# Layer 1 with fp16 plane pairs: two of every four probability tiles transposed by DMA, their low planes made on GpSimd

## The chip, the cores and the metric

One core of a Trainium2 chip runs the whole kernel. The metric is the device time of one execution in microseconds; the kernel before has a median of 682.38 us over 3 runs (681.85 to 683.33). Engine names are those of the profile: PE is TensorE's matmul and PEld its weight load, DVE is VectorE, ACT is ScalarE, POOL is GpSimd, SP is SyncE, which issues the DMAs.

## What is computed

Four images x of 256 channels and 1024 pixels (32 x 32), all in float32. Layer 0 is a position attention with a residual; layer 1 is a group norm, an attention of 4 heads of 64 channels and a projection with a residual:

```python
# layer 0
S = softmax(einsum('bcn,bcm->bnm', Wb @ x, Wc @ x))          # 1024 x 1024 per image
y = gamma * einsum('bcm,bnm->bcn', Wd @ x, S) + x
# layer 1
hn = group_norm(y, 32 groups)
q, k, v = (w @ hn + b for w, b in ((wq, bq), (wk, bk), (wv, bv)))   # 4 heads x 64
attn = softmax(einsum('bhdq,bhdk->bhqk', q, k) * 64 ** -0.5)        # 1024 x 1024 per head
out = y + wp @ einsum('bhqk,bhdk->bhdq', attn, v) + bp
```

To keep float32 accuracy, every operand of a matmul is split into a high part and a low part, and a product is two or three matmuls on them.

## The kernel before

**Tiles.** Layer 0 has 8 tiles per image and layer 1 has 32 (4 heads x 8), each 128 queries by 1024 keys. A layer-1 image runs 32 steps. Tiles are ordered so that four tiles in a row (4j to 4j+3) are 512 queries of one head: they make half a head, and their values product av j is computed in steps 4j+4 to 4j+7, a quarter (four matmuls of 512 columns) per step.

**One tile in layer 1.** PE computes the scores into one of two PSUM buffers (`scores1`), two steps ahead. DVE takes the row maximum (`row_max`), ACT the exponential with the row sum (`exp`), DVE the reciprocal of the sum (`recip`), POOL multiplies the tile by it (`normalise`). PE transposes the tile in eight 128 x 128 pieces into the PSUM pair `trans` (`transpose_tile`), ACT copies it out as the high part (`trans_high`), DVE subtracts for the low part (`trans_low`). PE then multiplies both parts with the stacked values (`values`). In the kernel before these parts are `pt_hi` and `pt_lo` in float32r.

**Layer 0** already turns its tiles by DMA: POOL writes the high fp16 plane (`high_plane`), DVE the low one (`plane_low`), SP issues one DMA transpose per plane (`turn`), and ACT and DVE widen the result to `pt_hi` and `pt_lo`.

**Order.** There is no scheduler. Each engine executes its instructions in the order in which they are written in its block, and semaphores tie the engines together. In layer 1 the table `STEPS1` says which groups PE adds in which step: projections of q and k for the next image (`next_qk0` to `next_qk6`, `qk7`), of v (`v0` to `v3`), the output projection, and the av quarters. In a step s of layer 1 the order is:

- PE: scores of tile s+2 (they wait for exp of tile s), transposes of tile s, the groups of `STEPS1[s]`, the av quarter last.
- ACT: put away a finished av, `trans_high` of tile s, exp of tile s+2, other groups' high parts.
- DVE: reciprocal of tile s+1, other groups of step s-1, row maximum of tile s+2, `trans_low` of tile s, av of step s-1.
- POOL: normalise tile s+1, then pieces of the group norm or of an output split.
- SP: it restacks each finished q or k chunk with four DMAs (`restack`), loads and stores.

The line numbers in rows are those of the kernel before: L979 row maximum, L739 exp, L984 reciprocal, L626 normalise, L1444 transposes, L749 and L997 high and low part of a transposed tile, L1410 all matmuls, L466 restack, L478 and L481 the layer-0 DMA transposes.

Of the kernel before, what the change touches and what calls it, by code (L numbers as in the profile page):

```python
# [21 lines left out]
F32 = mybir.dt.float32  # L22
F32R = mybir.dt.float32r
# [5 lines left out]
P = 128  # L29
IMAGES = 4  # L30
C = 256
# [28 lines left out]
PARTS0_FIRST = ["d0", "d1", "d2", "d3", "av0", "av1", "next_a0", "next_a1", "next_a2", "next_a3"]  # L60
# [165 lines left out]
def halves_before(t1):  # L226

    return 2 * t1 - TILES_LAYER0
# [19 lines left out]
def build(nc, x, weights, vecs, out):  # L248
    y_dram = nc.dram_tensor("y_scratch", (IMAGES, KT, P, N), F32, kind="Internal").ap()
    ctx = ExitStack()  # L250
    with ctx:
# [36 lines left out]
        pt_hi = sb("pt_hi", [P, 2, NT, H], F32R)  # L288
        pt_lo = sb("pt_lo", [P, 2, NT, H], F32R)
# [26 lines left out]
        v_st = sb("v_st", [P, NT, HEADS, 2, HD], F32R)  # L316
# [66 lines left out]
        pool_steps = sem("pool_steps")  # L383

# [49 lines left out]
        def _(sp):  # L434
# [5 lines left out]
            def load_x(i):  # L440
                for half in range(X_HALVES):
# [1312 lines left out]
```

## Time and profile before

| | us |
|---|---|
| median of 3 runs | 682.38 |
| the profiled execution | 682.95 |
| its span, first to last instruction | 681.0 |
| PE busy | 668.9 (98%) |
| DVE busy | 560.4 (82%) |
| ACT busy | 455.7 (67%) |
| POOL busy | 231.2 (34%) |

Layer 0 ends and layer 1 begins at about 242 us. PE reads as busy nearly throughout because matmuls are pipelined: a 512-column float32r matmul is recorded as 390 ns, while the next one starts about 228 ns after it. How long PE really takes is therefore read from the starts in the timeline, and whether an engine sets the pace is read from the gaps between starts on the others. The granted TensorE clock is 1.00 (2.4 GHz) over the whole span.

### The profile page before, as it was taken

How to read it: one execution, taken by the hardware profiler on the slowest of the kernel's cores; microseconds unless marked ns; L12 is line 12 of the kernel's file. 1: busy time of each engine (PE TensorE's matmuls, PEld its weight loads, DVE VectorE, ACT ScalarE, POOL GpSimd, SP SyncE). 2: the span in 40 equal slices, each digit the busy share in tenths (PEclk: the TensorE clock that was granted, in tenths of full speed). 3: DMA queues.
4: the chain of work that ended last, by engine and by line, in shares of the span. 5: the costliest groups of instructions: out<-in, count | busy, mean ns of one | idle time of the engine just before them, and what ended most of it. 6: DMA issues, size and time to landing. Idle time of an engine off the chain costs nothing.

```text
span 681.0 us, 11125 instructions
## 1 busy us (share of the span) xinstructions
PE 668.9 (98%) x3668; PEld 568.5 (83%) x3668; DVE 560.4 (82%) x910; ACT 455.7 (67%) x790; POOL 231.2 (34%) x216
## 2 busy tenths in 40 slices
PE   8989999999999899999999999999999999999997
PEld 7878888888888778888888888888888888988886
DVE  4787768768678478998888899888899888889996
ACT  5563435435435167988787788777789778778884
POOL 0130211201125024565233465242546433334531
PEclk9999999999999999999999999999999999999999
DMA  7476856645645957001656010367110265301001
GB/s 227 85 134 188 170 99 138 155 100 128 165 97 123 213 141 203 1 1 48 146 119 185 17 47 1 93 155 193 54 54 8 58 157 126 92 16 47 1 32 62
DMA packets 96714, 69.50 MB, mean 102 GB/s; under 512 B 71072, under 2 KB 73376, under 8 KB 96672
## 3 DMA queue, kind: packets, MB, share of 16 engines
q1 hardware_dynamic: 96672, 68.97, 41.8%
q8 instruction: 22, 0.36, 0.2%
q14 instruction: 20, 0.16, 0.1%
HBM read 18.62 MB, written 8.39 MB: 40 GB/s over the span
## 4 chain that ended last, share of the span: by engine, by line
PE 86%; DVE 5%; issue 3%; ACT 2%; POOL 2%; DMA 1%; SPq 1%; POOLq 0%; DVEq 0%; ACTq 0%
PE acc L1410 36%; PE scores L1410 26%; PE trans L1444 16%; PE trans L1410 8%; DVE negmax L979 1%; ACT prob L739 1%; DMA x_raw<-in_x 1%; POOL planes L638 1%; DVE pt_lo L997 1%; ACT pt_hi L749 1%; DVE pt_lo L1168 1%; DMA turned<-planes 0%; POOL y_in L649 0%; SPq L466 0%; DVE qk L1132 0%
## 5 line engine op out<-in xcount | busy, mean ns | idle before, releaser
L626 POOL TENSOR_SCALAR prob<-prob,rsum 128x1024 f32<-128x1024 f32 x127 | 142.8, 1124 | 256.7 <-DVE rsum L984 256.7
L739 ACT ACTIVATE prob<-scores,negmax 128x1024 f32<-128x1024 f32 x160 | 178.9, 1118 | 74.4 <-DVE negmax L979 72.9
L979 DVE TENSOR_REDUCE negmax<-scores 128x1 f32<-128x1024 f32 x160 | 194.0, 1213 | 17.8 <-PE scores L1410 16.6
L749 ACT ACTIVATE pt_hi<-trans 128x512 fp32r<-128x512 f32 x256 | 139.6, 594 | 63.9 <-PE trans L1444 63.3
L997 DVE TENSOR_TENSOR pt_lo<-trans,pt_hi 128x512 fp32r<-128x512 f32 x256 | 163.5, 680 | 1.0 <-ACT pt_hi L749 0.6
L1410 PE MATMUL scores<-k_st,q_st 128*128 128x512 f32 x512 | 137.9, 391 | 0.7 <-issue 0.7
L1444 PEld LDWEIGHTS trans<-ident,prob 128*128 128x128 f32 x1024 | 117.7, 140 | 22.5 <-issue 4.2
L1444 PE MATMUL trans<-ident,prob 128*128 128x128 f32 x1024 | 134.6, 273 | 1.2 <-DVE pt_lo L997 1.1
L1410 PEld LDWEIGHTS scores<-k_st,q_st 128*128 128x128 f32 x512 | 95.7, 188 | 21.6 <-issue 1.2
L1410 PE MATMUL acc<-pt_hi,v_st 128*128 128x512 f32 (+1 forms) x264 | 106.8, 407 | 0.6 <-DVE pt_lo L997 0.6
L1410 PE MATMUL acc<-pt_lo,v_st 128*128 128x512 f32 (+1 forms) x264 | 101.0, 385 | 0.0
L638 POOL TENSOR_SCALAR planes<-prob,rsum 128x1024 f16<-128x1024 f32 x32 | 36.7, 1146 | 164.9 <-DVE rsum L984 161.6
L1410 PEld LDWEIGHTS acc<-pt_hi,v_st 128*128 128x128 f32 x264 | 49.8, 189 | 7.8 <-DVE pt_lo L997 0.8
L812 ACT ACTIVATE pt_hi<-turned 128x1024 fp32r<-128x1024 f16 x32 | 33.8, 1057 | 33.3 <-DMA turned<-planes 33.3
L1410 PEld LDWEIGHTS acc<-pt_lo,v_st 128*128 128x128 f32 x264 | 49.9, 189 | 7.1
L984 DVE RECIPROCAL rsum<-rowsum 128x1 f32<-128x1 f32 x160 | 25.8, 161 | 31.8 <-ACT prob L739 27.2
L1012 DVE SCALAR_TENSOR_TENSOR planes<-prob,rscaled,planes 128x1024 f16<-128x1024 f32 x32 | 41.5, 1296 | 12.6 <-POOL planes L638 11.9
L1410 PE MATMUL scores<-x_hi,a_hi 128*128 128x512 f32 x128 | 50.0, 391 | 0.0
L1410 PE MATMUL scores<-x_hi,a_lo 128*128 128x512 f32 x128 | 49.9, 390 | 0.0
L1410 PE MATMUL scores<-x_lo,a_hi 128*128 128x512 f32 x128 | 49.8, 389 | 0.0
L739 ACT ACTIVATION_READ_ACCUMULATOR prob<-scores,negmax 128x1 f32 x160 | 31.7, 198 | 0.0
L1410 PE MATMUL acc<-pt_hi,d_hi 128*128 128x512 f32 x72 | 28.1, 390 | 2.1 <-DVE qk L1132 2.1
(163 smaller groups left out, 1028.0 us busy)
## 6 DMA issues: line engine op xcount, KB each, us to landing
k_st<-qk SPq DMA_DIRECT2D x64, 256.0 KB, 4.7
q_st<-qk SPq DMA_DIRECT2D x64, 128.0 KB, 2.4
x_raw<-in_x SPq DMA_DIRECT2D x8, 512.0 KB, 5.2
y_out<-in_x SPq DMA_DIRECT2D x16, 256.0 KB, 3.3
y_scratch<-y_out SPq DMA_DIRECT2D x16, 256.0 KB, 2.3
y_in<-y_scratch SPq DMA_DIRECT2D x4, 1024.0 KB, 7.5
y_res<-y_scratch SPq DMA_DIRECT2D x16, 256.0 KB, 3.7
out<-y_res SPq DMA_DIRECT2D x14, 256.0 KB, 2.1
```

What stands on the lines that cost most here:

```text
L626: nc.gpsimd.tensor_scalar(p, p, rsum[:, t % 2:t % 2 + 1], 1.0, ALU.mult, ALU.mult)\
L638: nc.gpsimd.tensor_scalar(planes[:, t % PLANE_SLOTS, 0, :], prob[:, t % 2, :], rsum[:, t % 2:t % 2 + 1], PROB_SCALE, ALU.mult, ALU.mult)\
L739: nc.scalar.activation(prob[:, t % 2, :], scores[:, t % 2, :], ACT.Exp, bias=negmax[:, t % 2:t % 2 + 1], scale=1.0, accum_out=rowsum[:, t ...
L749: nc.scalar.activation(pt_block(pt_hi, (t // 4) % 2, t, h), trans[:, h, :].rearrange("p (j n) -> p j n", n=P), ACT.Copy).then_inc(pt_high, 1)
L812: nc.scalar.activation(pt_tile(pt_hi, t), turned[t % TURN_SLOTS][:, 0, :, :], ACT.Copy, scale=1.0 / PROB_SCALE).then_inc(pt_high, 1)
L979: nc.vector.tensor_reduce(negmax[:, t % 2:t % 2 + 1], scores[:, t % 2, :], AX_X, ALU.max, negate=True).then_inc(max_ready, 1)
L984: nc.vector.reciprocal(rsum[:, t % 2:t % 2 + 1], rowsum[:, t % 2:t % 2 + 1]).then_inc(rsum_ready, 1)
L997: nc.vector.tensor_tensor(pt_block(pt_lo, slot, t, h), trans[:, h, :].rearrange("p (j n) -> p j n", n=P), pt_block(pt_hi, slot, t, h).bitc ...
L1012: nc.vector.scalar_tensor_tensor(planes[:, t % PLANE_SLOTS, 1, :], prob[:, t % 2, :], rscaled[:, t % 2:t % 2 + 1], planes[:, t % PLANE_SLO ...
L1168: nc.vector.tensor_scalar(pt_tile(pt_lo, t), turned[t % TURN_SLOTS][:, 1, :, :], 1.0 / PROB_SCALE, None, ALU.mult).then_inc(pt_split, 1)
L1410: ins = nc.tensor.matmul(dst, w, m, start=(starts and n == 0), stop=(stops and n == len(pairs) - 1))
L1444: ins = nc.tensor.transpose(trans[:, h, b * P:(b + 1) * P], prob[:, t % 2, j * P:(j + 1) * P], ident[:, :])
```

## The change

Probabilities (`pt16`) and stacked values (`v_st`) of layer 1 become pairs of fp16 planes. Tiles 0 and 2 of every four (`TURNED`) no longer go through PE: ACT writes their high plane, POOL subtracts for the low plane, and SP issues one DMA transpose of both planes straight into `pt16`. Tiles 1 and 3, and the last four tiles of the last image, go through PE as before, with fp16 results. Four tile buffers replace two. To fit fp16, the normalise multiplies by 32768, and wv is scaled by a bound that is computed on the chip once: POOL works on weights and norm factors after tile 4 of image 0 (`value_factors`), PE adds one small group `vb`, DVE computes the scales (`value_scales`) between the last `turned_low` of image 0 and its results, and only then is wv split. The av results are scaled back where they are put away. SP's part of layer 1 is written out step by step, with the transpose of a step ahead of the restacks.

```diff
+TURNED = (0,2,)
+LOW_ON_VECTOR = ()
...
+            def turn1(i, t):
+                sp.wait_ge(low_plane1[t % 4 in LOW_ON_VECTOR], lows_before(i, t) + 1)
+                if t % 4 == TURNED[0]:
+                    sp.wait_ge(acc_done, GROUP_CREDIT + slot_free(i, t) + 1)
+                sp.dma_start_transpose(
+                    pt16[:, (t // 4) % 2, :, :, (t % 4) * P:(t % 4 + 1) * P].rearrange("p a j n -> p (a j) n"),
+                    flat(planes[:, turn1_slot(t), :, :])).then_inc(turned1[turn1_slot(t)], 16)
...
+            def plane1_low(i, t):
+                pool.wait_ge(high_plane1, turned_before(i, t) + 1)
+                nc.gpsimd.tensor_tensor(planes[:, turn1_slot(t), 1, :], prob1(t), planes[:, turn1_slot(t), 0, :],
+                                        ALU.subtract).then_inc(low_plane1[False], 1)
...
             for t in range(T0_IMAGE):
                 high_plane(0, t)
+                if t == 4:
+                    value_factors()
...
                     if s + 1 < T1_IMAGE - DVE_TILES or not plan.last:
                         normalise(T1_BASE + T1_IMAGE * i, s + 1)
+                    if is_turned(i, s) and s % 4 not in LOW_ON_VECTOR:
+                        plane1_low(i, s)
...
+            def plane1_high(i, t):
+                d = turned_before(i, t)
+                if d < 2:
...
+                else:
+                    act.wait_ge(turned1[d % 2], 16 * (d // 2))
+                act.wait_ge(prob_ready, T1_BASE + T1_IMAGE * i + t + 1)
+                nc.scalar.activation(planes[:, d % 2, 0, :], prob1(t), ACT.Copy).then_inc(high_plane1, 1)
...
-                    trans_high(t1, s, before)
-                    if s + LAG < T1_IMAGE or not plan.last:
-                        exp(t1, s + LAG)
+                    if is_turned(i, s):
+                        plane1_high(i, s)
+                    else:
+                        trans_high(i, s)
+                    if s + LAG < T1_IMAGE:
+                        exp1(i, s + LAG)
...
             for t in range(T0_IMAGE - TURN_LAG, T0_IMAGE):
                 turned_low(0, t)
+            value_scales()
             for a in range(2):
                 result0(0, a)
...
-                    trans_low(t1, s)
+                    if not is_turned(i, s):
+                        trans_low(i, s)
...
                 if part == 0:
-                    pe.wait_ge(pt_split, SPLIT_CREDIT + halves_before(t1) + 8 * (j + 1))
+                    pe.wait_ge(pt_split, SPLIT_CREDIT + splits_before(i, 4 * (j + 1)))
+                    for t in TURNED:
+                        pe.wait_ge(turned1[turn1_slot(4 * j + t)], turn1_count(i, 4 * j + t))
...
-                    transpose_tile(t1, s, plan.last)
+                    if not is_turned(i, s):
+                        transpose_tile(i, s)
```

What this does to the order on three engines follows. On PE, in image 0, around the first quarter of an av group: before, each step has its transposes between the scores and the av quarter.

```order
L1410 MATMUL scores<-k_st,q_st 128x512 [waits exp_ready]
L1410 MATMUL scores<-k_st,q_st 128x512 x3
L1444 MATMUL trans<-ident,prob 128x128 [waits pt_split,prob_ready]
L1444 MATMUL trans<-ident,prob 128x128 x3
L1444 MATMUL trans<-ident,prob 128x128 [waits pt_split]
L1444 MATMUL trans<-ident,prob 128x128 x3
L1410 MATMUL acc<-pt_hi,v_st 128x512 [waits acc_evac,pt_split]
```

The same place after the change, with the scores of the step behind it (`turned1_even` and `turned1_odd` count landed DMA transposes; `pt` is `pt16`):

```order
L1604 MATMUL scores<-k_st,q_st 128x512 [waits exp_ready]
L1604 MATMUL scores<-k_st,q_st 128x512 x3
L1604 MATMUL acc<-pt,v_st 128x512 [waits turned1_odd,acc_evac,turned1_even,pt_split]
L1604 MATMUL acc<-pt,v_st 128x512 x3
L1604 MATMUL scores<-k_st,q_st 128x512 [waits exp_ready]
L1604 MATMUL scores<-k_st,q_st 128x512 x3
L1638 MATMUL trans<-ident,prob 128x128 [waits pt_split,prob_ready]
```

Step 4j+4 has no transposes left, its av quarter waits for two DMA transposes, and the scores of tile 4j+7 and the transposes of tile 4j+5 stand behind that quarter.

On POOL, in the first steps of layer 1: before, normalises follow each other.

```order
L626 TENSOR_SCALAR prob<-prob,rsum 128x1024 [waits rsum_ready] x7
L649 TENSOR_SCALAR y_in<-y_in,gn_now 128x512 [waits y_loaded,gn_affine]
L626 TENSOR_SCALAR prob<-prob,rsum 128x1024 [waits rsum_ready] x2
L399 TENSOR_TENSOR h_lo<-y_in,h_hi 128x512 [waits h_high]
```

After (`prob_more` holds tiles 2 and 3 of four; the TENSOR_TENSOR into `planes` is the low plane):

```order
L727 TENSOR_SCALAR prob<-prob,rsum 128x1024 [waits rsum_ready] x2
L734 TENSOR_TENSOR planes<-prob,planes 128x1024 [waits high_plane1]
L727 TENSOR_SCALAR prob_more<-prob_more,rsum 128x1024 [waits rsum_ready] x2
L734 TENSOR_TENSOR planes<-prob_more,planes 128x1024 [waits high_plane1]
L727 TENSOR_SCALAR prob<-prob,rsum 128x1024 [waits rsum_ready] x2
```

The low plane of a turned tile stands behind the normalise of the tile after it.

On SP, in image 0 of layer 1, steps 21 to 27: before, the restacks of q and k chunks stand alone.

```order
L466 DMA q_st<-qk 64x512 [waits acc_evac]
L466 DMA q_st<-qk 64x512 x3
L466 DMA k_st<-qk 64x2x512 [waits acc_evac]
L466 DMA k_st<-qk 64x2x512 x3
L466 DMA k_st<-qk 64x2x512 [waits acc_evac]
L466 DMA k_st<-qk 64x2x512 x3
L565 DMA out<-y_res 128x512 [waits acc_evac]
```

After:

```order
L660 DMA_TRANSPOSE pt<-planes 128x16x128 [waits acc_done,low_plane1_pool]
L553 DMA q_st<-qk 64x512 [waits acc_evac]
L553 DMA q_st<-qk 64x512 x3
L660 DMA_TRANSPOSE pt<-planes 128x16x128 [waits low_plane1_pool]
L553 DMA k_st<-qk 64x2x512 [waits acc_evac]
L553 DMA k_st<-qk 64x2x512 x3
L553 DMA k_st<-qk 64x2x512 [waits acc_evac]
L553 DMA k_st<-qk 64x2x512 x3
L660 DMA_TRANSPOSE pt<-planes 128x16x128 [waits acc_done,low_plane1_pool]
```

Restacks and transposes now share SP's queue, in the order of the steps.

## Rows read from the trace of the kernel before

**Rows 1.** Windows: layer 0, then image 2 of layer 1; columns as named.

```profile
core 0: us, PE busy (x) PEld busy (x) DVE busy (x) ACT busy (x) POOL busy (x), PEclk, DMA share, GB/s
0.00:242.00 242.00, 235.09 (x1138) 198.24 (x1138) 170.86 (x272) 108.41 (x157) 44.77 (x48) 1.00 0.64 146
457.70:567.30 109.60, 109.56 (x634) 93.63 (x633) 97.62 (x158) 87.84 (x161) 48.97 (x44) 1.00 0.33 86
```

**Rows 2.** Groups by line and form, 260 to 672 us; busy us, mean ns, idle.

```profile
L997 DVE TENSOR_TENSOR pt_lo<-trans,pt_hi 128x512 fp32r<-128x512 f32 x249 | 159.1, 680 | 1.0 <-ACT pt_hi L749 0.6
...
L1302 DVE TENSOR_TENSOR v_st<-acc,v_st 128x256 fp32r<-128x256 f32 x30 | 11.3, 419 | 7.0 <-ACT v_st L887 6.9
```

**Rows 3.** PE timeline, one step of image 1: start us, duration us, instruction.

```profile
442.89 1.07 PE L1410 MATMUL scores<-k_st,q_st 128*128 128x512 f32 x4
443.80 1.03 PE L1444 MATMUL trans<-ident,prob 128*128 128x128 f32 x8
444.59 0.48 PE L1410 MATMUL acc<-o_hi,wp_hi 128*128 128x512 f32 x1
```

**Rows 4.** ACT timeline of the same step.

```profile
444.43 1.09 ACT L749 ACTIVATE pt_hi<-trans 128x512 fp32r<-128x512 f32 x2 [1.31 <-PE trans L1444]
445.40 1.12 ACT L739 ACTIVATE prob<-scores,negmax 128x1024 f32<-128x1024 f32 x1
```

**Rows 5.** DVE timeline: a k chunk put away, and the next reciprocal.

```profile
443.16 0.75 DVE L1132 SCALAR_TENSOR_TENSOR qk<-acc,vec,qk 128x512 fp32r<-128x512 f32 x1 [0.41 <-ACT qk L795]
...
446.64 0.16 DVE L984 RECIPROCAL rsum<-rowsum 128x1 f32<-128x1 f32 x1 [0.23 <-ACT prob L739]
```

**Rows 6.** POOL timeline, layer 1: normalise, and operations with one and two inputs.

```profile
293.13 0.18 POOL L660 TENSOR_TENSOR gn_sqdev<-gn_dev 128x2 f32<-128x2 f32 x1
...
447.01 1.13 POOL L626 TENSOR_SCALAR prob<-prob,rsum 128x1024 f32<-128x1024 f32 x1 [2.94 <-DVE rsum L984]
...
452.69 1.29 POOL L403 TENSOR_TENSOR o_lo<-o_sum,o_hi 128x512 fp32r<-128x512 f32 x1
...
510.42 0.77 POOL L649 TENSOR_SCALAR y_in<-y_in,gn_now 128x512 f32<-128x512 f32 x1
```

**Rows 7.** SP timeline: the last DMA transposes of layer 0, a k restack.

```profile
222.72 1.29 SPq L478 DMA_TRANSPOSE turned<-planes  x1
224.06 1.33 SPq L481 DMA_TRANSPOSE turned<-planes  x1
...
462.91 3.40 SPq L466 DMA_DIRECT2D k_st<-qk  x4
```

**Rows 8.** DMA issues of the page: KB each, median us to landing.

```profile
x_raw<-in_x SPq DMA_DIRECT2D x8, 512.0 KB, 5.2
...
turned<-planes SPq DMA_TRANSPOSE x64, 3.3
```

**Rows 9.** DVE timeline: reciprocals of tile 3 (image 0), 15, 16, 19 (image 2), 31 (image 3).

```profile
254.06 0.15 DVE L984 RECIPROCAL rsum<-rowsum 128x1 f32<-128x1 f32 x1
...
511.68 0.17 DVE L984 RECIPROCAL rsum<-rowsum 128x1 f32<-128x1 f32 x1 [0.25 <-ACT prob L739]
...
514.23 0.16 DVE L984 RECIPROCAL rsum<-rowsum 128x1 f32<-128x1 f32 x1
...
522.50 0.16 DVE L984 RECIPROCAL rsum<-rowsum 128x1 f32<-128x1 f32 x1
...
667.77 0.17 DVE L984 RECIPROCAL rsum<-rowsum 128x1 f32<-128x1 f32 x1 [0.26 <-ACT prob L739]
```

**Rows 10.** POOL timeline, layer 0, image 0: the normalise of tile 5.

```profile
41.68 1.12 POOL L638 TENSOR_SCALAR planes<-prob,rsum 128x1024 f16<-128x1024 f32 x1 [2.96 <-DVE rsum L984]
```

**Rows 11.** PE timeline: first value matmul of image 0, first scores of image 1.

```profile
45.49 0.47 PE L1410 MATMUL trans<-pt_hi,d_hi 128*128 128x512 f32 x1 [1.77 <-DVE d_lo L1095]
...
61.93 0.39 PE L1410 MATMUL scores<-x_hi,a_hi 128*128 128x512 f32 x1
```

**Rows 12.** DVE timeline: first two low parts that the scores of image 1 need.

```profile
59.80 1.27 DVE L1095 TENSOR_TENSOR a_lo<-acc,a_hi 128x512 fp32r<-128x512 f32 x2
```

More of the change, by code:

```diff
@@ L589, in _ @@
+                if plan.has("next_qk6"):
+                    restack(plan, "next_qk6")
+            for i in range(IMAGES):
                 image1(i)
-            image1(IMAGES - 1)
+            load_residual(IMAGES - 1, 1)
             for side, name in enumerate(EPILOGUE_OUT):
@@ L743, in trans_high, with exp1 @@
-            def trans_high(t0, t, av_before):
-                if t % 4 == 0 and av_before is not None:
-                    wait_acc(av_before)
+                nc.scalar.activation(dst, scores[:, t % 2, :], ACT.Exp, bias=negmax[:, t % 2:t % 2 + 1], scale=1.0,
+                                     accum_out=rowsum[:, column:column + 1]).then_inc(exp_ready, 1)
+            def exp1(i, s):
+                if plan1(i).first and s < 2:
+                    act.wait_ge(low_plane, T1_BASE + s + 1)
+                elif plan1(i).first and s < 4:
+                    wait_acc(plan0(IMAGES - 1).number("av1"))
+                elif (s - 4) % 4 in TURNED:
+                    act.wait_ge(low_plane1[s % 4 in LOW_ON_VECTOR], lows_before(i, s - 4) + 1)
+                else:
+                    act.wait_ge(transposed, TRANS_CREDIT + 2 * passed_before(i, s - 4) + 2)
+                exp(T1_BASE + T1_IMAGE * i, s, prob1(s), s % 4)
@@ L928, in evacuate @@
                         output_rows(plan, name, i)
-            exp(T1_BASE, 1, True)
+            exp1(0, 1)
             def image1(i):
@@ L1571, in _ @@
                     project_d(0, D_STEPS.index(s))
+            pe.wait_ge(v_factors, 10 + KT)
+            group(plan0(0), "vb", [(v_spread[:, k, :], wv_size[:, k, :]) for k in range(KT)], slice(0, C))
             d_split(0)
@@ L1683, in side_values @@
                 if part == 0:
[L1685 removed]
+                    pe.wait_ge(pt_split, SPLIT_CREDIT + splits_before(IMAGES - 1, T1_IMAGE - 2 * (1 - side)))
                 group(plan_epilogue, EPILOGUE_AV[side], [
[L1687 to L1688 removed]
+                    (v_st[:, b, HEADS - 1, :, :].rearrange("p v d -> p (v d)"), pt16[:, 1, plane, b, col(side, SIDE)])
+                    for b in range(NT) for plane in range(2)], slice(0, SIDE), part, parts)
             def image1(i):
```

286 lines of the change are left out of this document (194 added, 92 removed).

## The prediction

> **What bounds the kernel now.** I read the busy shares by windows first. In layer 0 PE is busy 235.1 of 242 us; in image 2 of layer 1, 109.56 of 109.6 us, with DVE at 97.6, ACT at 87.8 and POOL at 49.0 [rows 1]. A busy PE may be pipelined records, so I then read the starts. In one step four score matmuls take 443.80 - 442.89 = 0.91 us and the eight transposes 0.79 [rows 3]; an av quarter is four matmuls of the score form, 0.91. A plain step is 2.6 us of PE.
>
> There is a second bound, almost as tight: exp, reciprocal, row maximum, next exp. DVE's in-order stream takes the reciprocal of tile s+1 before the maximum of tile s+2, so this chain is serial. Its price is 514.23 - 511.68 = 2.55 us per tile [rows 9]. Four plain tiles, with one finished av put away, take 522.50 - 511.68 = 10.8 us. A q or k chunk lengthens the chain by DVE's wait and work, 0.41 + 0.75 = 1.16 us [rows 5]; a v chunk I take alike (two operations of 0.42, and a wait) [rows 2]. So a faster PE alone can't bring a plain group of four tiles under about 10.8 us: the transposes that leave were hardly slower than the chain.
>
> **Part by part: the work.** 62 of 128 tiles lose eight transposes (62 x 0.79 = 49 us of PE) and two `trans_low` (62 x 2 x 0.68 = 84 us of DVE) [rows 2, 3]. ACT swaps two halves (1.09 us, [rows 4]) for one plane of about the same size: nothing. POOL gains 62 low planes. No row has that operation. Its lower bound is a one-input pass over 1024 columns, 1.13; its upper bound two 512-column subtractions, 2 x 1.29 = 2.58. A two-element TENSOR_TENSOR costs 0.18, so a second half costs 1.29 - 0.18 and I take 2.40, near the row of its own kind [rows 6]. POOL then has 49.0 + 16 x 2.4 = 87 us per image, under the pace. fp16 matmuls of 512 columns I take at the float32r cadence; no row shows them.
>
> **The new wait.** This decides the time. In step 4j+4 PE has no transposes: after the scores of tile 4j+6 it reaches the first quarter of av j, and that waits until tile 4j+2 has landed. Behind it in PE's stream stand the scores of tile 4j+7 and the transposes of tile 4j+5, so exp and the whole chain wait too. From the reciprocal of tile 4j+3 (time 0):
>
> - 0.37 until POOL's normalise of tile 4j+3 starts (447.01 - 446.64) [rows 5, 6], 1.13 for it; the high plane of tile 4j+2 runs on ACT meanwhile.
> - 2.40 for the low plane of 4j+2, which stands behind that normalise: 3.90.
> - The transpose of both planes to landing. Two single planes stood 224.06 - 222.72 = 1.34 apart at issue, and one lands after 3.3: 4.64 [rows 7, 8]. Bounds: 3.3 if the second plane is free, 5.2 if it lands like a 512 KB load. Landed at 8.54.
> - av quarter 0.91, scores of 4j+7 0.91 [rows 3]: 10.36.
> - Transposes of 4j+5 to ACT's copy 444.43 - 443.80 = 0.63, copy to exp 0.97 [rows 3, 4], exp to the next reciprocal 446.64 - 445.40 = 1.24 [rows 4, 5]: 13.2.
>
> That is the reciprocal of tile 4j+7, so four tiles take at least P = 13.2 us, where a plain group takes 10.8. Evacuations that lengthen a group today fall into this wait and cost nothing while it lasts.
>
> **Sum for layer 1.** From tile 3 of image 0 to tile 31 of image 3 are 31 groups, today 667.77 - 254.06 = 413.7 us [rows 9]. Each now takes the larger of P and its chain:
>
> - six groups with three q, k or v chunks (tiles 3 to 7 of images 1 to 3, and across three image ends): 10.8 + 3 x 1.16 = 14.3, together 85.8;
> - six groups with two chunks and an output block of 0.75 (the size of [rows 5]): 13.9, together 83.4;
> - the other 19 at P: 250.8.
>
> 420.0, or +6.3. At each image end SP must issue three k restacks of 3.4 us [rows 7], four q restacks and five double transposes of 2.6 us in some 25 us, in order; ACT's next chunk waits for a restacked slot. I take 2 us for each of three ends (0 to 5): +6. Layer 1: +12.3.
>
> **Layer 0.** POOL's weight and norm factors follow tile 4 of image 0: seven operations of a few columns at about 0.2 us; two of 0.77, one of 1.29, and two of 128 columns, 0.3 to 0.4 each; with handovers about 5.0 [rows 6]. POOL idles 2.96 there [rows 10], so the high plane of tile 5 comes 2.1 late, and `plane_low`, then `d_low` of step 5 behind it on DVE. PE waits for that `d_low` at 45.49 after 1.77 idle [rows 11], so nothing covers it: +2.1, and 0.2 for the two `vb` matmuls.
>
> The scales stand on DVE ahead of the results of image 0: some ten operations, of which six have 256 columns at 0.42 [rows 2], two half that, one 512 at 0.64 [rows 12], with a handover to ACT and back of 0.7: 4.5 us. The low parts that the scores of image 1 need end at 59.80 + 1.27 = 61.07, the scores start at 61.93 [rows 11, 12]: 0.86 of cover, +3.6. Layer 0: +5.9, between 2 and 9 (reciprocal over 256 columns has no row). The wv split that leaves the lead-in frees 0.6 us of DVE while PE is the bound: nothing.
>
> Sum: 682.95 + 12.3 + 5.9 = 701.15 for the profiled execution; the median is 0.57 lower, so **701**.
>
> **A rule against the low estimate.** Single planes land after 3.3 us with 1.3 us between issues [rows 7, 8]. The Trainium skill, Advanced Engine Details and Errata, section X-Bar Transpose (TRN2), says that transposing DMAs are as fast as regular ones; by the 512 KB load at 5.2 us, P would be 13.8 and the sum some 11 us higher. The rows of single planes are of the operation itself, so I stay with 4.64.
>
> **Rivals.**
>
> 1. *The tiles land in time: faster.* If low plane and transpose together take 5.7 us or less instead of 7.04, P is below 11.9 and layer 1 gives back more than the additions cost. With a one-input price on POOL (1.13) and a second plane for nothing (3.3), the wait is gone: 14 groups at 10.8, five two-chunk groups at 13.1 and the twelve heavy ones make 385.9, or -27.8; with +5.9 the end is 660.5. For it: PE at 99.96% is really relieved by 49 us. Against it: the only two-input rows on POOL cost 1.29 per 512 columns.
> 2. *The clock falls.* PE would idle some 4 us per plain group (4.2 to 8.5 after the reciprocal). Before, its granted clock is 1.00, 2.4 GHz, in every window, with no idle stretch that long [rows 1, 11]. If it stood at 1.2 GHz after each such wait, quarter, scores and transposes would take 0.91 + 0.91 + 0.6 us more: 2.4 x 19 groups = 46, an end near 747. The Trainium skill, TensorE: Matmul & The Clock Gate, section HAM oscillation, has waits between bursts of matmuls cost the clock each time; no run here shows it yet, and PE works most of each period.
> 3. *SP's queue sets the image ends.* If restacks behind transposes hold ACT for 5 us and the heavy groups for 1 us more: 9 + 12 us above the forecast, 722. For it: 32 us of issue in some 25 us. Against it: the restacked chunks are needed only steps later.
>
> **How the numbers follow.** The forecast (waiting for the landing, 690 to 715) has 0.60, rival 1 with all its shades below 681 0.22, rival 2 0.06, rival 3 0.07; the rest, near no change, 0.05. A measurement of this kernel can tell about 0.2% from no change. Ends: P at 11.9 (either bound alone) gives about 683, both 660; P at 14.5 (2.58 for the low plane, and a landing 1.1 us later) gives about 730. I leave out the lower tail of rival 1 and most of rival 2: 672 to 728. Slower 0.73, same 0.05, faster 0.22.
>
> **What would show it.** Right: av matmuls on `pt16` waiting for the DMA of `planes`, some 2 to 4 us in most groups; reciprocals of tiles 4j+3 about 13 us apart in the middle of an image, alike in plain and heavy groups; PE idle some 50 us in layer 1; POOL's low plane near 2.4 us and DMA transposes landing after about 4.6; scores of image 1 starting near 68 instead of 61.93. Wrong: tiles landed before PE asks, groups of 10 to 11 us, and the low plane near 1.2; or a granted clock below 1.00.

## The result and the profile after

The changed kernel takes 758.54 us (median of 4 runs, 756.52 to 761.26), the kernel before 682.86 beside it (681.85 to 684.57): ratio 1.110, 95% interval 1.107 to 1.114. The forecast was 701. The profiled execution took 756.52 us, its span is 753.9, against 681.0 before. Three marks divide the 72.9 us between: layer 1's first reciprocal comes at 256.83 us instead of 245.82 (+11.0), tile 3's 8.35 us later instead of 8.24 (+0.1), and from there to tile 31 of image 3 stand the 31 groups of the prediction:

```profile
265.18 0.15 DVE L1141 RECIPROCAL rsum<-rowsum 128x1 f32<-128x1 f32 x1
...
740.71 0.16 DVE L1141 RECIPROCAL rsum<-rowsum 128x1 f32<-128x1 f32 x1 [0.29 <-ACT prob_more L873]
```

That is 475.5 us, where it was 413.7 [rows 9]: +61.8. The windows view of the two stages (columns as in [rows 1]):

```profile
0.00:256.80 256.80, 244.61 (x1158) 205.11 (x1159) 176.89 (x283) 109.17 (x160) 53.20 (x60) 0.97 0.61 140
265.20:740.70 475.50, 394.35 (x1909) 270.23 (x1908) 305.30 (x485) 331.14 (x549) 310.83 (x226) 0.92 0.65 136
```

PE, busy throughout before, now lacks 475.50 - 394.35 = 81 us of layer 1, POOL is at 65% of it, and the granted clock has fallen to 0.92. Three lines of the page and one of the DMA view: the av matmuls wait 42.9 us for landed tiles, POOL's low planes take 2.14 us, the double transposes land after a median of 4.3.

```profile
L1604 PE MATMUL acc<-pt,v_st 128*128 128x512 f16 (+1 forms) x528 | 144.3, 402 | 53.3 <-DMA pt<-planes 42.9
...
L734 POOL TENSOR_TENSOR planes<-prob,planes 128x1024 f16<-128x1024 f32 x31 | 66.3, 2139 | 14.6 <-ACT planes L906 14.1
L734 POOL TENSOR_TENSOR planes<-prob_more,planes 128x1024 f16<-128x1024 f32 x31 | 66.4, 2141 | 1.2 <-ACT planes L906 0.3
...
pt<-planes SPq DMA_TRANSPOSE x62, 4.3
```

**A plain group** (image 2, tiles 15 to 19; 14.45 us). DVE, POOL, SP and PE in the timeline:

```profile
563.95 0.17 DVE L1141 RECIPROCAL rsum<-rowsum 128x1 f32<-128x1 f32 x1 [0.29 <-ACT prob_more L873]
...
575.70 1.23 DVE L1135 TENSOR_REDUCE negmax<-scores 128x1 f32<-128x1024 f32 x1 [3.37 <-PE scores L1604]
...
578.40 0.16 DVE L1141 RECIPROCAL rsum<-rowsum 128x1 f32<-128x1 f32 x1 [0.29 <-ACT prob_more L873]
```

```profile
564.32 1.12 POOL L727 TENSOR_SCALAR prob_more<-prob_more,rsum 128x1024 f32<-128x1024 f32 x1 [0.37 <-DVE rsum L1141]
565.40 2.13 POOL L734 TENSOR_TENSOR planes<-prob_more,planes 128x1024 f16<-128x1024 f32 x1
```

```profile
567.56 1.71 SPq L660 DMA_TRANSPOSE pt<-planes  x1
```

```profile
567.18 1.28 PE L1604 MATMUL scores<-k_st,q_st 128*128 128x512 f32 x4
572.08 1.89 PE L1604 MATMUL acc<-pt,v_st 128*128 128x512 f16 x4 [3.62 <-DMA pt<-planes]
573.41 2.25 PE L1604 MATMUL scores<-k_st,q_st 128*128 128x512 f32 x4
575.47 1.06 PE L1638 MATMUL trans<-ident,prob 128*128 128x128 f32 x8
576.37 1.03 PE L1604 MATMUL acc<-pt,v_st 128*128 128x512 f16 x4
```

The chain of the prediction is there link by link: low plane from 1.45 to 3.58 us behind the reciprocal, PE goes on at 8.1. New is what follows: the quarter behind the wait takes 1.89 us and the scores 2.25, a step later they take 1.03 and 1.28. That is the lower of the two clock levels, 1.2 GHz; the granted clock stands in the column behind POOL (columns as in [rows 1]):

```profile
572.00:575.40 3.40, 3.32 (x8) 2.00 (x9) 0.16 (x1) 0.13 (x2) 2.95 (x3) 0.51 0.59 162
575.50:578.50 3.00, 3.00 (x19) 2.12 (x18) 2.52 (x5) 2.31 (x5) 0.00 (x0) 1.00 0.50 93
```

Of the 14 waits for landing in the trace, nine, of 3.59 to 5.21 us, are followed by a quarter of 1.80 to 1.89 us, and five, of 0.57 to 2.30 us, by one of 1.02 or 1.03.

**Groups 1** (18.5 to 20.3 us in images 0 to 2). POOL in image 2:

```profile
530.55 1.13 POOL L727 TENSOR_SCALAR prob_more<-prob_more,rsum 128x1024 f32<-128x1024 f32 x1
536.76 0.76 POOL L783 TENSOR_SCALAR y_in<-y_in,gn_now 128x512 f32<-128x512 f32 x1 [5.08 <-DMA y_in<-y_scratch]
...
539.82 2.15 POOL L734 TENSOR_TENSOR planes<-prob_more,planes 128x1024 f16<-128x1024 f32 x1
```

The norm chunk waits 5.08 us for the next image's y, and the low plane of tile 6 stands behind it. SP, in order, had issued that load only at 528.05, behind a transpose and a restack.

**Image ends** (groups 7, 19.1 to 20.2 us). POOL's low plane of tile 26, then SP, then PE:

```profile
484.79 2.14 POOL L734 TENSOR_TENSOR planes<-prob_more,planes 128x1024 f16<-128x1024 f32 x1
```

```profile
486.96 2.85 SPq L660 DMA_TRANSPOSE pt<-planes  x1
489.85 7.88 SPq L553 DMA_DIRECT2D k_st<-qk  x8
```

```profile
502.45 1.18 PE L1604 MATMUL scores<-k_st,q_st 128*128 128x512 f32 x4 [3.29 <-DMA k_st<-qk]
```

The k chunk was put away by 484.54 us; SP stood at the transpose of tile 26, whose low plane wasn't ready until 486.9, and PE then waited for k.

**Layer 0.** POOL behind tile 4 of image 0, then PE:

```profile
38.07 1.05 POOL L744 TENSOR_SCALAR v_bound<-vec 128x2 f32<-128x2 f32 x1
...
39.70 2.35 POOL L747 TENSOR_SCALAR y_in<-y_in 128x512 f32<-128x512 f32 x1
42.02 1.93 POOL L748 TENSOR_SCALAR y_in<-y_in 128x512 f32<-128x512 f32 x1
...
46.80 1.12 POOL L772 TENSOR_SCALAR planes<-prob,rsum 128x1024 f16<-128x1024 f32 x1
```

```profile
46.87 2.08 PE L1604 MATMUL trans<-y_in 128*128 128x256 f32 x4 [4.32 <-POOL y_in L760]
...
50.61 0.76 PE L1604 MATMUL trans<-pt_hi,d_hi 128*128 128x512 f32 x1 [1.66 <-DVE d_lo L1255]
...
71.19 0.49 PE L1604 MATMUL scores<-x_hi,a_hi 128*128 128x512 f32 x1 [0.30 <-DVE a_lo L1255]
```

`value_factors` runs from 37.74 to 46.8, 9.1 us. The first value matmul comes 5.1 us later than in [rows 11], the scores of image 1 9.3 later.

### The profile page after: what moved, and what is told of

Read it like the earlier page. It is cut to its first block, busy times and chain, and to the rows that moved or that the text cites. A ratio compares the mean times of both kernels' runs of the same rounds, so it can differ in the third digit from the quotient of the medians.

```text
span 753.9 us, 10033 instructions
## 1 busy us (share of the span) xinstructions
PE 655.6 (87%) x3176; PEld 488.9 (65%) x3176; DVE 496.6 (66%) x795; ACT 452.3 (60%) x728; POOL 369.5 (49%) x290
## 4 chain that ended last, share of the span: by engine, by line
PE 44%; DMA 14%; POOL 12%; ACT 8%; issue 7%; SPq 7%; DVE 6%; POOLq 0%; ACTq 0%; DVEq 0%
PE acc L1604 18%; PE scores L1604 16%; DMA pt<-planes 8%; POOL planes L734 6%; PE trans L1604 6%; SPq L553 4%; PE trans L1638 3%; POOL prob_more L727 3%; DMA y_in<-y_scratch 2%; ACT prob_more L873 2%; ACT pt L894 2%; DMA k_st<-qk 2%; SPq L660 2%; DVE negmax L1135 2%; ACT prob L873 2%
## 5 line engine op out<-in xcount | busy, mean ns | idle before, releaser
L1604 PE MATMUL acc<-pt,v_st 128*128 128x512 f16 (+1 forms) x528 | 144.3, 402 | 53.3 <-DMA pt<-planes 42.9
L1604 PE MATMUL scores<-k_st,q_st 128*128 128x512 f32 x512 | 174.5, 465 | 12.4 <-DMA k_st<-qk 7.8
L873 ACT ACTIVATE prob<-scores,negmax 128x1024 f32<-128x1024 f32 x96 | 107.1, 1116 | 120.4 <-DVE negmax L1135 120.4
L1604 PEld LDWEIGHTS acc<-pt,v_st 128*128 128x128 f16 x528 | 45.9, 102 | 117.1 <-issue 71.6
L727 POOL TENSOR_SCALAR prob<-prob,rsum 128x1024 f32<-128x1024 f32 x64 | 71.9, 1123 | 101.7 <-DVE rsum L1141 101.6
L894 ACT ACTIVATE pt<-trans 128x512 f16<-128x512 f32 x132 | 71.9, 594 | 72.6 <-PE trans L1638 72.6
L727 POOL TENSOR_SCALAR prob_more<-prob_more,rsum 128x1024 f32<-128x1024 f32 x63 | 70.7, 1123 | 54.7 <-DVE rsum L1141 54.5
L1159 DVE TENSOR_TENSOR pt<-trans,pt 128x512 f16<-128x512 f32 x132 | 85.0, 682 | 3.9 <-ACT pt L894 3.5
L873 ACT ACTIVATE prob_more<-scores,negmax 128x1024 f32<-128x1024 f32 x64 | 71.4, 1116 | 14.1 <-DVE negmax L1135 13.7
L734 POOL TENSOR_TENSOR planes<-prob,planes 128x1024 f16<-128x1024 f32 x31 | 66.3, 2139 | 14.6 <-ACT planes L906 14.1
L734 POOL TENSOR_TENSOR planes<-prob_more,planes 128x1024 f16<-128x1024 f32 x31 | 66.4, 2141 | 1.2 <-ACT planes L906 0.3
```

The costliest lines, as they stand in the source:

```text
L727: nc.gpsimd.tensor_scalar(prob1(t), prob1(t), rsum[:, t % 4:t % 4 + 1], PROB_SCALE, ALU.mult, ALU.mult)\
L734: nc.gpsimd.tensor_tensor(planes[:, turn1_slot(t), 1, :], prob1(t), planes[:, turn1_slot(t), 0, :], ALU.subtract).then_inc(low_plane1[Fals ...
L873: nc.scalar.activation(dst, scores[:, t % 2, :], ACT.Exp, bias=negmax[:, t % 2:t % 2 + 1], scale=1.0, accum_out=rowsum[:, column:column + ...
L894: nc.scalar.activation(pt16_block(0, t, h), trans[:, h, :].rearrange("p (j n) -> p j n", n=P), ACT.Copy).then_inc(pt_high, 1)
L1159: nc.vector.tensor_tensor(pt16_block(1, t, h), trans[:, h, :].rearrange("p (j n) -> p j n", n=P), pt16_block(0, t, h), ALU.subtract).then_ ...
L1604: ins = nc.tensor.matmul(dst, w, m, start=(starts and n == 0), stop=(stops and n == len(pairs) - 1))
```

## The experiments

All profiles are read by one measure: the time from the reciprocal of tile 4j+3 to that of tile 4j+7, summed over the images by j (group 7 crosses an image end and occurs three times). The start of layer 1 and the groups are those of the profiled execution, the last column is the median of all runs.

| kernel | layer 1 starts | 0 | 1 | 2 to 4 | 5 | 6 | 7 | 31 groups | median us |
|---|---|---|---|---|---|---|---|---|---|
| before | 245.8 | 58.7 | 58.0 | 139.4 | 55.4 | 58.5 | 43.7 | 413.7 | 682.86 |
| changed | 256.8 | 58.7 | 71.6 | 170.8 | 57.0 | 58.7 | 58.8 | 475.5 | 758.54 |
| e_pe_only | 257.1 | 58.0 | 58.0 | 141.6 | 56.0 | 58.0 | 44.6 | 416.2 | 696.90 |
| e_free | 257.5 | 54.0 | 56.5 | 129.1 | 54.0 | 54.3 | 44.6 | 392.6 | 673.81 |
| e_load | 258.3 | 54.0 | 71.7 | 135.4 | 54.9 | 57.9 | 58.5 | 432.4 | 711.51 |
| e_warm | 258.6 | 59.2 | 71.1 | 185.7 | 55.3 | 58.5 | 57.4 | 487.1 | 769.76 |
| e_warm14 | 258.2 | 59.3 | 68.7 | 160.1 | 56.8 | 57.4 | 57.6 | 460.0 | 744.14 |
| e_yearly | 257.3 | 68.2 | 58.4 | 172.1 | 57.1 | 59.2 | 58.1 | 473.1 | 755.59 |
| e_yprev | 257.9 | 61.2 | 57.0 | 173.9 | 55.2 | 57.5 | 60.1 | 464.9 | 746.33 |
| e_restack | 258.2 | 59.3 | 72.5 | 169.8 | 56.9 | 65.4 | 46.4 | 470.2 | 752.84 |
| e_late0 | 251.8 | 59.4 | 71.1 | 173.8 | 57.2 | 58.9 | 57.5 | 477.9 | 752.43 |
| e_tiles01 | 259.5 | 54.4 | 69.9 | 148.6 | 64.6 | 58.1 | 61.6 | 457.2 | 734.49 |
| e_all_pool | 246.7 | 54.4 | 63.0 | 148.6 | 64.3 | 55.3 | 54.1 | 439.7 | 713.34 |
| e_all_dve | 249.3 | 58.6 | 62.9 | 151.4 | 57.7 | 60.5 | 43.2 | 434.4 | 705.67 |
| e_one | 259.1 | 54.5 | 59.3 | 135.2 | 54.9 | 58.1 | 45.8 | 407.8 | 689.01 |
| e_one_all | 248.3 | 54.5 | 60.0 | 135.1 | 54.9 | 54.9 | 44.8 | 404.2 | 676.14 |

The theory: layer 1 loses by PE's wait for the second turned tile and by what the change puts into in-order streams ahead of older work, layer 0 by its own additions. The rivals are told with each run: A and B are the two theories of the text that was put on record before it.

**e_pe_only**, no tile turned:

```diff
-TURNED = (0,2,)
+TURNED = ()
```

> No tile of layer 1 is turned by DMA: all 128 go through PE with fp16 planes; the scaling of wv in layer 0 stays, and so do the four tile buffers and SP's step order. Theory A (layer 1 loses by the wait for the landed tile, layer 0 by its own additions): layer 1 is back at groups of about 10.8 us and 31 groups near 414 us (475.5 in the changed kernel); layer 0 keeps its +11.0 us; total 694 (690 to 698). Rival B (fp16 matmuls or fp16 PSUM reads are themselves slower, or SP's new order costs): 31 groups take 430 us or more, total over 708. Granted clock by A: 1.00 throughout layer 1.

Ratio 1.020 (1.018 to 1.022). Layer 0 keeps its 11.3 us, the groups cost 2.5 more than before at a granted clock of 1.00: A. Turning tiles costs 475.5 - 416.2 = 59.3 us.

**e_tiles01**, tiles 0 and 1 turned:

```diff
-TURNED = (0,2,)
+TURNED = (0, 1)
```

> Tiles 0 and 1 of every four are turned instead of 0 and 2, so that the second turned tile's low plane and transpose start one tile (2.5 to 3 us) earlier; the number of turned tiles, of low planes on POOL and of double transposes stays 62 of each. Theory A (the landing of the second turned tile, 8.1 us after the reciprocal of tile 4j+3, and the clock that falls after the wait for it, set the groups): the tile lands about 5.3 us after that reciprocal, PE waits about 1 us or less, plain groups fall from 14.1 to between 10.8 and 12 us, 31 groups from 475 to 380 to 420, total 665 to 705. Rival B (the load on SP's queue and on POOL, which is unchanged, sets them): 31 groups stay over 450, total over 735.

Ratio 1.073 (1.069 to 1.077). Groups 2 to 4 fall by 22 us to 12.4 each, and one wait for landing is left, of 0.5 us; groups 1 fall by 1.7, 5 and 7 grow. The total lies above A's range and just below B's: the landing is one part of the loss, the in-order queues another. PE's waits for POOL's normalise ahead of transposes rise from 8.0 to 28.6 us. The profiled execution, at 740.88 us, is the slowest of its four (729.97 the fastest), so the table's sum for this kernel is on the high side.

**e_warm and e_warm14**, PE kept at work in the wait:

```diff
+                if part == 0 and j in (2, 3, 4):
+                    bank_free(plan, name)
+                    for _ in range(26):
+                        nc.tensor.matmul(group_out(plan, name, slice(0, P)), ident[:, :], ident[:, :], start=True, stop=True)
```

> The changed kernel, but PE multiplies the 128x128 identity by itself 26 times into the group's own bank just before it asks for the landed tile, in av groups 2, 3 and 4 of each image (12 groups); the later start of the group overwrites that. 26 such products take 3.1 us at 2.4 GHz (0.12 each, as the warm-up at the start shows), and PE waits some 3.6 us there. Theory A (the clock falls to 1.2 GHz after the wait, and quarter, scores and transposes behind it run at half speed): granted clock 1.00 in these groups, their quarter takes about 1.0 instead of 1.86 to 1.89 us, scores 1.27 instead of 2.25, and they fall from 14.1-15.8 us to about 12.8; 12 groups by 1.3 to 2: total 15 to 24 us lower, 735 to 743. Rival B (the clock is no part of it: PE is not the bound there): the twelve groups keep their length within 0.3 us, total 755 to 760.

e_warm became slower, 1.127, outside both ranges: my price of the filler was half the true one. PE in image 1:

```profile
451.69 5.96 PE L1840 MATMUL acc<-ident 128*128 128x128 f32 x52
457.50 1.03 PE L1604 MATMUL acc<-pt,v_st 128*128 128x512 f16 x4
458.17 1.28 PE L1604 MATMUL scores<-k_st,q_st 128*128 128x512 f32 x4
```

> As e_warm, with 14 products of the identity instead of 26. In e_warm each of them took 0.23 us (26 in 5.96), not the 0.12 that I had read from rows that count two for each product; so the filler outlasted the wait of 3.6 us by 2.3. 14 take 3.2 us and end just inside the wait. Theory A (the fallen clock costs what the changed kernel's groups lie above 12.8): granted clock 1.00, av quarter 1.03 and scores 1.27 us behind the wait, groups 2, 3 and 4 of all images between 12.6 and 13.2 us, their sum 151 to 158 instead of 170.9; total 740 to 746. Rival B (the landing itself comes later when PE runs on, or the clock only moves the wait): the sum of these groups stays over 165, total over 752.

With 14 products (ratio 1.090, 1.088 to 1.092), the same place:

```profile
453.66 3.29 PE L1840 MATMUL acc<-ident 128*128 128x128 f32 x28
457.34 1.02 PE L1604 MATMUL acc<-pt,v_st 128*128 128x512 f16 x4 [0.39 <-issue]
458.01 1.30 PE L1604 MATMUL scores<-k_st,q_st 128*128 128x512 f32 x4
```

The quarter behind the wait is at full speed, and groups 3 and 4 go from 116.7 to 104.2, 13.0 each, where P at full clock predicts 13.2. Seven of these eight had had a slow quarter; they fall by 13.3 us, 1.9 each, and the eighth, which had run at full clock, grows by 0.9. Groups 2 grow by 1.7 in sum: in images 1 and 2 they already ran at full clock, PE waits there for a bank, and the filler stands in the way. A, but for those groups.

**e_yearly and e_yprev**, the load of y elsewhere in SP's stream:

```diff
-                    if s == 3 and not plan.last:
+                    if s == 0 and not plan.last:
```

> The changed kernel, but SP issues the load of the next image's y right behind the transpose of tile 0 of each image instead of behind that of tile 2, two restacks and their waits. Theory A (in groups j = 1 of images 0 to 2 POOL stands 5.1 us at its first norm chunk for that load, and the low plane of tile 6 behind it comes 5.9 us late): the wait is gone, these three groups fall from 18.5-20.3 to 13 to 14.5 us, total 13 to 18 us lower, 740 to 746. Rival B (the load is late because the DMA engines are crowded, not by its place in the queue): POOL still waits over 3 us there and the total stays within 5 us of 758.

Ratio 1.107 (1.101 to 1.113), 3 us less, which the runs (751.86 to 760.59) do not tell from no change. POOL's wait goes (groups 1: -13.2), but the load now runs beside the transpose of tile 2, which lands late (groups 0: +9.5). Neither theory alone: the loss moved.

```diff
-                    if s == 3 and not plan.last:
-                        sp.wait_ge(h_split, 4 * i + 4)
-                        load_y(i + 1)
+                    if s == 20 and i + 2 < IMAGES:
+                        sp.wait_ge(h_split, 4 * i + 8)
+                        load_y(i + 2)
```

> The load of y for image i+2 is issued in step 20 of image i, when its buffer has just come free, instead of in step 3 of image i+1; that of image 1 ahead of the first transpose of layer 1. e_yearly, with the load in step 0, took 13.2 us from groups 1 and gave 9.5 us back in groups 0, whose second transpose then landed late beside the load. Theory A (the load costs by its place, either as a wait on POOL or beside a transpose on the DMA engines): groups 1 stay near 58 in sum (71.6 in the changed kernel) and groups 0 near 59; total 742 to 748. Rival B (a load of 1 MB costs some 3 to 4 us wherever it stands, since transposes load the DMA engines all the time): groups 5 become longer by 3 to 4 us each for images 0 and 1 and the total is 750 to 756.

Ratio 1.093 (1.090 to 1.095). Groups 1 are back at 57.0; POOL's norm chunk has no wait left:

```profile
539.29 1.12 POOL L730 TENSOR_SCALAR prob_more<-prob_more,rsum 128x1024 f32<-128x1024 f32 x1
540.39 0.77 POOL L786 TENSOR_SCALAR y_in<-y_in,gn_now 128x512 f32<-128x512 f32 x1
```

Groups 5 did not grow: A. The load's place in the queue cost 12 us.

**e_restack**, restacks ahead of transposes in steps that have both:

```diff
-                    if is_turned(i, s):
+                    if is_turned(i, s) and not restacked(plan, s):
                         turn1(i, s)
...
                             store(plan, name, i)
+                    if is_turned(i, s) and restacked(plan, s):
+                        turn1(i, s)
```

> In the steps in which SP both restacks a chunk of the next image's q or k and issues a transpose, the restack goes first (steps 22, 24, 26, 30). Theory A (SP's order costs the image ends: at 484.54 the k chunk was ready, SP stood at the transpose of tile 26 until 486.96 and issued it for 2.85 us, and PE later waited 3.29 us for that k): the wait of the scores for k at the end of an image goes, groups 7 of images 0 to 2 fall from 19.0-20.2 to 15 to 16.5 us; transposes behind restacks land up to 3 us later, +1 to 2 us in groups 5 and 6; total 746 to 751. Rival B (the DMA engines are full: k arrives late because the transposes' many small packets share them): groups 7 stay over 18 us, total 755 to 761.

Ratio 1.104 (1.101 to 1.108). Groups 7 fall from 58.8 to 46.4, so the order was their cause; groups 6 rise by 6.7, more than I gave, since the transposes now land behind the restacks, and the total ends 1.8 us above A's range. SP, same place as above:

```profile
485.35 3.43 SPq L553 DMA_DIRECT2D k_st<-qk  x4
488.82 4.53 SPq L660 DMA_TRANSPOSE pt<-planes  x1
```

**e_late0**, layer 0's additions moved:

```diff
+            value_factors()
             for t in range(T0_IMAGE):
                 high_plane(0, t)
-                if t == 4:
-                    value_factors()
...
-            value_scales()
             for a in range(2):
                 result0(0, a)
...
+            value_scales()
```

> In layer 0 the bounds on weights and norm factors are computed on POOL before tile 0 of image 0 (POOL idles there until 20.84 us; the weights have landed at 13.1) instead of after tile 4, and the small group vb, the scales on DVE and the high part of wv follow the last group of image 0 instead of standing ahead of its results. Theory A (layer 0's +11.0 us are POOL's 9.1 us in the middle of image 0 and DVE's 5.3 us ahead of the results, both exposed): the first value matmul of image 0 starts near 45 us (50.61 in the changed kernel, after 2.08 us of vb), the scores of image 1 near 62 to 64 instead of 71.19, layer 1 starts 7 to 10 us earlier; total 748 to 752. Rival B (the additions only move and delay image 1 by the same 5.3 us on DVE and about 1 us of PE): layer 1 starts 3 to 5 us earlier; total 753 to 756.

Ratio 1.100 (1.098 to 1.103). The first value matmul is at 45.42 and the scores of image 1 start at 64.13 us, as A has it; but layer 1 starts only 5.0 earlier, as B has it, in a trace whose clock is 0.94 to 0.95 in two stretches of layer 0. In three later kernels with the same layer 0 it starts 7.5 to 10.1 earlier, as A has it. Kernels with the changed kernel's layer 0 start layer 1 at 256.8 to 259.5, so one trace does not decide between the two. DVE's part is not hidden; its row maximum of image 1 waits behind it:

```profile
65.67 1.75 DVE L1340 RECIPROCAL y_in<-y_in 128x256 f32<-128x256 f32 x1
...
70.19 1.22 DVE L1134 TENSOR_REDUCE negmax<-scores 128x1 f32<-128x1024 f32 x1
```

**e_free**, what the change could reach if turning cost nothing (for e_free and e_load, the av matmuls read a buffer of layer 0):

```diff
-                    for t in TURNED:
-                        pe.wait_ge(turned1[turn1_slot(4 * j + t)], turn1_count(i, 4 * j + t))
...
-                group(plan, name, [(v_st[:, b, j % 4, :, :].rearrange("p v d -> p (v d)"), pt16[:, j % 2, plane, b, :])
+                group(plan, name, [(v_st[:, b, j % 4, :, :].rearrange("p v d -> p (v d)"), turned[0][:, plane, b // 4 * 4:b // 4 * 4 + 4, :])
```

and without `turn1`, `plane1_high` and `plane1_low`.

> Tiles 0 and 2 of every four are neither transposed nor turned in layer 1: their planes on ACT and POOL, the DMA transposes and PE's wait for them are left out, and the av matmuls, of the same number and shape, read a fixed fp16 buffer of layer 0 instead (so the outputs are not the reference's). It is what the change could reach at best, with landing, planes and DMA load for nothing; layer 0's +11 us stay. Theory A (exp, reciprocal and row maximum follow each other in 2.55 us per tile, so PE's 49 us buy little): plain groups 10.3 to 11 us, chunk groups as before, 31 groups 390 to 415, total 671 to 696. Rival B (PE was the bound and its 49 us would have been the gain, had the tiles landed in time): 31 groups 360 to 385, total 641 to 666.

Ratio 0.986 (0.984 to 0.989): A. A plain group of DVE's reciprocals:

```profile
510.47 0.17 DVE L1135 RECIPROCAL rsum<-rowsum 128x1 f32<-128x1 f32 x1
...
513.09 0.16 DVE L1135 RECIPROCAL rsum<-rowsum 128x1 f32<-128x1 f32 x1 [1.33 <-ACT prob L869]
...
515.71 0.16 DVE L1135 RECIPROCAL rsum<-rowsum 128x1 f32<-128x1 f32 x1
...
518.33 0.16 DVE L1135 RECIPROCAL rsum<-rowsum 128x1 f32<-128x1 f32 x1 [0.68 <-ACT prob_more L869]
...
520.95 0.16 DVE L1135 RECIPROCAL rsum<-rowsum 128x1 f32<-128x1 f32 x1
```

2.62 us per tile, 10.48 per group, and PE busy for 364.7 of 392.6 us: 49 us of transposes bought 23.6 (416.2 to 392.6). The chain of exp, reciprocal and maximum was the second bound: DVE waits for exp, and PE has time left.

**e_load**, all the work, but PE does not wait for it:

```diff
-                    pt16[:, (t // 4) % 2, :, :, (t % 4) * P:(t % 4 + 1) * P].rearrange("p a j n -> p (a j) n"),
+                    turn_junk[:, turn1_slot(t), :, :],
```

with the two edits of e_free's diff, where planes and `turn1` stay.

> All work of the changed kernel is done, planes, low planes on POOL and 62 double transposes, but the transposes write to an unused buffer and the av matmuls read a fixed fp16 buffer, so that PE waits for no landing (the outputs are not the reference's). Theory A (PE's wait for the landing, with the clock that falls behind it, sets groups 2 to 4): their sum falls from 170.9 to 128 to 145; the places where SP's queue and POOL's wait for y set the time (groups 1 and 7, 71.6 and 58.8) stay over 65 and 54; total 715 to 732. Rival B (POOL's low planes and the DMA load hold up the chain even without that wait): groups 2 to 4 stay over 155, total over 742.

Ratio 1.040 (1.036 to 1.043): A, with a total 3.5 us under its range. Groups 1 and 7 keep their 71.7 and 58.5, so PE's wait for the landing is no part of them. Groups 2 to 4 are at 135.4 though the DMA engines are even busier (share 0.72, by windows):

```profile
266.62:699.03 432.41, 379.27 (x1912) 259.39 (x1911) 303.81 (x487) 330.79 (x550) 310.34 (x226) 0.96 0.72 149
```

**e_all_pool and e_all_dve**, the three fixes (y load as in e_yprev, restacks as in e_restack, layer 0 as in e_late0) with tiles 0 and 1 turned; the second with

```diff
-LOW_ON_VECTOR = ()
+LOW_ON_VECTOR = (0, 1)
```

> Together: tiles 0 and 1 of every four turned (e_tiles01), the load of y for image i+2 in step 20 of image i (e_yprev), layer 0's additions moved (e_late0), restacks ahead of transposes in steps that have both (e_restack). If the savings add: from 734.5 of e_tiles01, -12 for the load, -6 for layer 0, -8 for the restacks (groups 7 -14, groups 6 up to +6): 705 to 712. Theory A (what is left is POOL: 2.14 us of low plane ahead of each normalise, for which PE idles 1 to 2 us before transposes): groups 2 to 4 stay near 148, 31 groups 425 to 440, total 699 to 714. Rival B (the places are linked and what one gives another takes): total over 718.

Ratio 1.044 (1.041 to 1.046): A, at its upper end; the savings nearly add. POOL's low planes still stand ahead of normalises (groups 5 at 64.3; the next run, with none on POOL, has 57.7).

> As e_all_pool, but the low planes of the turned tiles are made on DVE (which the tables allow) instead of POOL. Theory A (POOL's low planes delay the normalises and so PE): groups 2 to 4 fall from about 148 to 132 to 140, 31 groups 405 to 425, total 680 to 700; it does not beat the kernel before by more than 2 us, since the chain of exp, reciprocal and maximum holds the pace at 10.8 us a group and layer 0 has 6 us more. Rival B (a low plane on DVE stands between maximum and reciprocal and lengthens that chain by 1.2 us for two tiles of four): groups 2 to 4 at 145 or more, total over 704.

Ratio 1.032 (1.029 to 1.034). Groups 2 to 4 did not fall, 151.4: B. On DVE a low plane takes 1.22 to 2.21 us, median 1.35, and stands in the chain.

**e_one and e_one_all**, one turned tile in four, alone and with the three fixes:

```diff
-TURNED = (0,2,)
+TURNED = (0,)
```

> Only tile 0 of every four is turned (31 tiles), tiles 1 to 3 go through PE. Its landing has about 5 us more cover than that of tile 2. Theory A (the loss is a matter of which tile lands last: a tile whose landing has three tiles of cover costs no wait): groups 2 to 4 near 136 to 141 (139.5 before, 129.1 with landing for nothing and two tiles out); SP's queue and the y wait remain in part, groups 1 and 7 between the kernel before and the changed kernel; 31 groups 415 to 430, total 693 to 712. Rival B (each transpose costs about the same, in SP's queue and on POOL, whichever tile it is): half of the loss, 31 groups 443 to 448, total 720 to 727.

Ratio 1.009 (1.007 to 1.010). 407.8 is below A's range, where B has 445: with these 31 tiles layer 1 loses nothing, its groups are now faster than before (407.8 against 413.7); what is left is layer 0. The loss came with the second tile: by its landing, which nothing covers (e_tiles01 and e_load show that part), and by what it adds to POOL's and SP's queues. This run takes out both at once; tile 2 alone was not run, so it does not divide them.

> e_one with the load of y in step 20 of the image before, layer 0's additions moved, restacks ahead of transposes in steps that have both. By theory A nothing of layer 1 waits any more: 31 groups 400 to 413 (392.6 with landing for nothing and two tiles out, 413.7 before), layer 1 starts at 247 to 252, total 675 to 688, about the kernel before (682.4). Rival B (transposes on SP's queue still hold back the restacks at the image ends and in image 0): 31 groups over 418, total over 693.

676.14 us (675.49 to 676.96), ratio 0.990 (0.989 to 0.992): a version that beats both kernels, at a granted clock of 1.00 in the groups. At av's first quarter PE no longer waits for a DMA:

```profile
418.62 1.28 PE L1611 MATMUL scores<-k_st,q_st 128*128 128x512 f32 x4
420.12 1.03 PE L1611 MATMUL acc<-pt,v_st 128*128 128x512 f16 x4 [0.22 <-DVE pt L1166]
```

## Why the prediction was wrong

The sign was right, and the wait for the landing came where it was forecast. What failed is the rest of the sum: it left the clock out, held groups 1 at P, and gave the image ends and layer 0 too little. Against the sum of the prediction, groups 1 took 18.8 us more, groups 2 to 4 12.4, groups 7 9.9, groups 5 and 6 together 5.9, groups 0 2.6 and layer 0 5.1. By differences of the table, layer 1's 413.7 becomes 475.5 so: +2.5 for fp16 (e_pe_only), -23.6 for the work that leaves (e_free), +39.8 for the planes, transposes and queues even if nobody waits for a landing (e_load), +43.1 for that wait with its clock. Of the 39.8, groups 1 and 7 hold 29; of the 43.1, groups 2 to 4 hold 35. The order of subtraction is a choice; the parts are not independent.

- **The wait for the landing: right.** Forecast 8.54 us after the reciprocal, measured 8.1; low plane 2.40 forecast, 2.14 measured; landing 4.64 forecast, median 4.3. Groups at full clock took 12.8, forecast P = 13.2. The Trainium skill's rule (Advanced Engine Details and Errata, section X-Bar Transpose (TRN2)) has transposing DMAs as fast as regular ones. The landing of 5.2 that I had worked out by it from the 512 KB load was too dear here; the rows of single planes were the better guide.
- **"2. The clock falls": held at 0.06, and it came.** Its price was 2.4 us a group; e_warm14 shows 1.9 in the seven groups that it brings back to full clock. Groups 2 to 4 took 170.8, forecast 12 x 13.2 = 158.4. I argued that PE works most of each period; the trace shows that this did not keep the clock up. The Trainium skill's TensorE: Matmul & The Clock Gate, section HAM oscillation, spoke for the rival, and this trace agrees with it in nine of 14 waits for landing.
- **"The other 19 at P": wrong for groups 1.** They took 71.6 where 4 x 13.2 = 52.8 was forecast, the largest single miss. Some 4 us of it are no wait: e_free, where no tile lands, has these groups at 56.5 (58.0 before), so their own chain is longer than P. I priced SP's queue at image ends alone and did not ask who waits for the y load that stands behind transposes in that queue. e_yprev shows the answer: POOL, and behind it the next low plane (71.6 to 57.0 with the load moved).
- **"I take 2 us for each of three ends": mis-sized.** Groups 7 were forecast at 42.9 + 6 and took 58.8. The cause that I named was right, but a restack does not only share SP's time, it waits behind a transpose that itself waits for POOL; e_restack takes 12.4 us out and gives 6.7 back in groups 6. This is rival 3, and it came together with the forecast, not instead of it.
- **Layer 0: +11.0, forecast +5.9 (2 to 9).** `value_factors` was priced at 5.0 us and took 9.1: maximum and minimum on POOL took 2.35 and 1.93 us, where I took 0.77 from a multiply-add of the same shape [rows 6]. The reciprocal of 256 columns, which had no row, took 1.75. PE idled 4.32 us in that stretch, and the clock fell there too (0.85 from 40 to 75 us, 1.00 before). The `vb` group, priced at 0.2 us, took 2.08 at the lower clock, but PE then still waited 1.66 for `d_low`, so it cost nothing more. Of the 11.0 us, 9.3 stand at the scores of image 1; the other 1.7 arise behind them, and no run divides those.
- **"Transposes were hardly slower than the chain": right,** and worth more than I drew from it: e_free puts the most the change could win, with layer 0's additions as they are, at 10 us.

## What to carry to other kernels

When work moves to a queue that runs in order, list every instruction behind it and who waits for that, loads included; two of the three largest misses here (groups 1 and 7) were older instructions that fell behind new ones. Price a wait of PE at both clock levels, and give the slow one a real chance whenever PE would idle where it never did before. And move only what has cover: one tile in four, with three tiles of work before its landing is needed, won 1% once the queues were put in order; two in four (0 and 2) lost 11%, and tiles 0 and 1 with the same order 3 to 4%. Tiles 0 and 2 with that order were not run.

## What the runs showed of the hardware

- A two-operation tensor_scalar on POOL, 128x512 float32, took 0.77 us with multiply and add, and 1.93 to 2.35 with maximum or minimum and multiply.
- A 128x128 float32 product of the identity took 0.23 us at full clock and counts as two records (26 as x52 in 5.96 us).
- Four fp16 matmuls of 512 columns let the next scores start after 0.68 us (566.50 to 567.18), but those then take 1.28 instead of 1.07 [rows 3]. e_pe_only, with fp16 in all of layer 1's av matmuls, gains nothing: its groups take 416.2 us, 413.7 before.
- SP's issue of a double transpose took 1.3 to 7.6 us in the changed kernel, median 1.9; its landing took 4.2 to 9.6.
